# The first stage of an attention and mixture-of-experts layer: the router as moving rows, GpSimd's work later, the first chunk in four loads and banks

## The reference

```
xn = layernorm(x)
out = x + attention(xn) + moe(xn)

attention: q, k, v = xn @ Wq + bq, xn @ Wk + bk, xn @ Wv + bv        (16 heads of 32)
           softmax(q k^T / sqrt(32) + alibi slope * distance, causal) v, then @ Wo + bo
moe:       router_in = norm_w * xn * rsqrt(mean(xn^2) + 1e-6)
           probs = softmax(router_in @ router_w.T)                   (8 experts)
           the two best experts, their shares normalised to 1
           y = 4 * sum over both of share * (silu(xn @ gate) * (xn @ up)) @ down
```

## Time and profile before

| | us |
|---|---|
| median of 3 runs (lowest, highest) | 2081.18 (2076.91, 2083.2) |
| the profiled execution's own time | 2078.22 |
| its span | 2076.2 |
| TensorE busy in the span | 1954.8 |
| VectorE, ScalarE, GpSimd busy | 1442.9, 1320.5, 1360.5 |

### The profile page before, as it was taken

How to read it: one execution, slowest core, us unless ns; L and a number is a source line. 1 busy time by engine, 2 the same in 40 slices (tenths; PEclk the granted TensorE clock), 3 DMA queues, 4 the chain that set the end, 5 groups by cost and what they waited for, 6 DMA issues and landing times. The chain is left out here.

```text
span 2076.2 us, 38386 instructions
## 1 busy us (share of the span) xinstructions
PE 1954.8 (94%) x8670; PEld 1418.8 (68%) x8671; DVE 1442.9 (69%) x3391; ACT 1320.5 (64%) x2603; POOL 1360.5 (66%) x1199
## 2 busy tenths in 40 slices
PE   5999999899999999999999999999969989999996
PEld 4888877666767767676766667677637666666664
DVE  6445455788888888888888888898778833333332
ACT  3323321798998989899898989999852323333332
POOL 4110112788888889888888888888867535555554
PEclk9999999899999999999999999999989999999999
DMA  6667767442423233242423324232117755555554
GB/s 219 213 223 265 240 198 223 122 114 54 120 53 100 74 81 93 68 104 53 103 71 81 94 73 100 53 86 68 34 52 231 229 156 97 99 93 100 95 97 71
DMA packets 118487, 243.94 MB, mean 117 GB/s; under 512 B 15920, under 2 KB 52656, under 8 KB 112144
## 3 DMA queue, kind: packets, MB, share of 16 engines
q1 hardware_dynamic: 100464, 206.09, 34.3%
q0 software_dynamic: 17984, 37.38, 10.3%
HBM read 139.28 MB, written 104.21 MB: 117 GB/s over the span
## 5 line engine op out<-in xcount | busy, mean ns | idle before, releaser
L1061 POOL TENSOR_TENSOR probs_lo<-probs,probs_hi 128x512 fp32r<-128x512 f32 x800 | 1013.5, 1296 | 168.3 <-ACT probs L1092 168.0
L1091 ACT ACTIVATE probs_hi<-s_ps 128x512 fp32r<-128x512 f32 x928 | 597.4, 644 | 93.7 <-DVE s_ps L1155 91.2
L1092 ACT ACTIVATE probs<-s_ps 128x512 f32<-128x512 f32 x960 | 595.5, 651 | 0.2 <-DVE s_ps L1155 0.2
L1134 DVE TENSOR_REDUCE m_part<-m_ps 128x1 f32<-128x512 f32 x744 | 490.7, 684 | 11.3 <-PE m_ps L1369 5.6
L1385 PE MATMUL s_ps<-q_st,k_st 100*128 100x512 f32 (+3 forms) x880 | 323.6, 409 | 35.2 <-ACT probs L1092 17.1
L1369 PE MATMUL m_ps<-k_st,q_st 98*128 98x512 f32 (+2 forms) x840 | 281.7, 377 | 0.0
L1403 PE MATMUL o_ps<-probs_hi,v_split 128*96 128x512 f32 (+3 forms) x748 | 279.0, 383 | 1.0 <-POOL probs_lo L1061 0.5
L1404 PE MATMUL o_ps<-probs_lo,v_split 128*96 128x512 f32 (+3 forms) x748 | 269.9, 364 | 0.0
L1131 DVE CUSTOM_DVE_ANT_0 m_ps<-m_ps,mask_row 128x128 f32<-128x128 f32 x496 | 241.6, 497 | 19.2 <-PE m_ps L1369 12.8
L1385 PEld LDWEIGHTS s_ps<-q_st,k_st 100*128 100x128 f32 x880 | 159.2, 190 | 128.4 <-ACT probs L1092 55.4
L1759 POOL DMA_INDIRECT out<-y,tile_rows x71 | 114.2, 1609 | 170.9 <-issue 99.8
(11 more groups left out here) (202 smaller groups left out, 3615.9 us busy)
## 6 DMA issues: line engine op xcount, KB each, us to landing
v_d<-v_rows SPq DMA_DIRECT2D x7, 3072.0 KB, 9.4
v_split<-v_d SPq DMA_DIRECT2D x22, 768.0 KB, 8.4
k_st<-k_hi_d SPq DMA_DIRECT2D x44, 256.0 KB
q_st<-q_hi_d SPq DMA_DIRECT2D x44, 256.0 KB
xs<-in_x SPq DMA_DIRECT2D x8, 1024.0 KB, 6.8
xn_d<-xs SPq DMA_DIRECT2D x8, 1024.0 KB, 11.4
q_hi_d<-qk_hi SPq DMA_DIRECT2D x32, 256.0 KB, 7.6
q_lo_d<-qk_lo SPq DMA_DIRECT2D x32, 256.0 KB, 7.9
```

Source lines behind the costliest of these rows:

```text
L1061: nc.gpsimd.tensor_tensor(*low_operands(u), ALU.subtract).then_inc(lo_ready_pool, 1)
L1091: nc.scalar.activation(probs_hi[:, P_SLOT[u]], scores, ACT.Exp, scale=SCALE)
L1092: nc.scalar.activation(scores if KIND[u] == "Q" else probs[:, P_SLOT[u]], scores, ACT.Exp, scale=SCALE).then_inc(p_ready, 1)
L1134: V.tensor_reduce(top, scores, AX.X, ALU.max).then_inc(m_taken, 1)
```

## The change

1. The router. `rw` is padded with zeros from 16 to 128 columns and becomes the stationary operand; x moves past it, 512 columns at a time: 4 k x 2 parts = 8 matmuls (`router_rows`). Row n of the result `pr` holds the products with weight column n. DVE copies it to SBUF (`take_rows`; `logit_rows` lies where the raw slopes were, so it waits for `al_ready`), PE turns it back with four transposes (`turn_logits`), and `route` reads the 16 columns of each block. The rows are made ahead of the value tiles and turned behind the second of them; in chunk 7 ahead of tile 4 and tile 6. `route` still follows the value tiles (chunk 7: tile 7 instead of 4).
2. POOL splits Wv, and does all behind it, only once chunk 1's x is normalised.
3. Chunk 0's x comes in four DMAs with a semaphore each; its statistics are taken block by block. Its four transpose groups go to four banks (the maxima's `mp` and the router's `pr` serve as the third and fourth), without waiting for x_lo.

```
-        rw = sb(ctx, "rw", [P, KD, 2 * E], F32R)
+        rw = sb(ctx, "rw", [P, KD, P], F32R)
+        def turned_x(k, first=False):
+            return (xt[:, 0], xt[:, 1], mp[:, :], pr[:, :])[k] if first else xt[:, k % 2]
 SP
-            sp.dma_start(xs[0][:, :, :], x_rows(0)).then_inc(x_loaded[0], 16)
+            for j in range(TPC):
+                sp.dma_start(xs[0][:, j], x[j * P:(j + 1) * P, :]).then_inc(x_first[j], 16)
 POOL
             pool.wait_ge(xn_ready, TPC)
-            for w in range(3):
-                w_low(w)
+            w_low(0)
+            w_low(1)
+            pool.wait_ge(xn_ready, 2 * TPC)
+            w_low(2)
             pool.wait_ge(al_loaded, 16)
 DVE, norm_stats (chunk 0)
                 for j in range(TPC):
+                    if first:
+                        dve.wait_ge(x_first[j], 16)
                     last = nc.vector.bn_stats(stats[:, j], xs[par][:, j])
 DVE
+            def take_rows(c):
+                dve.wait_ge(al_ready, 1)
+                dve.wait_ge(rows_scored, c + 1)
+                nc.vector.tensor_copy(logit_rows[:, :], pr[:, :]).then_inc(rows_taken, 1)
-                nc.vector.tensor_copy(halves[:, :, :], pr[:, 0:TPC * 2 * E].rearrange("p (j e) -> p j e", j=TPC)).then_inc(r_used, 1)
+                nc.vector.tensor_copy(halves[:, :, :], pr[:, :].rearrange("p (j n) -> p j n", j=TPC)[:, :, 0:2 * E]).then_inc(r_used, 1)
+            nc.vector.memset(rw[:, :, 2 * E:].bitcast(F32), 0.0)
 DVE, chunk
                     if last and g == G:
+                        take_rows(c)
+                    if last and g == G + 3:
                         route(c, par)
+                if not last:
+                    take_rows(c)
                 for j in range(TPC):
 PE
-            def router_tiles(c, par):
+            def router_rows(c, par):
+                pe.wait_ge(rw_ready, 1)
                 pe.wait_ge(r_used, c + 1)
+                for k in range(KD):
+                    for n, part in enumerate((x_hi, x_lo)):
+                        last = nc.tensor.matmul(pr[:, :], rw[:, k], part[par][:, k], start=(k == 0 and n == 0),
+                                                stop=(k == KD - 1 and n == 1))
+                last.then_inc(rows_scored, 1)
+            def turn_logits(c):
+                pe.wait_ge(rows_taken, c + 1)
                 for j in range(TPC):
...
+                    last = nc.tensor.transpose(pr[:, j * P:(j + 1) * P], logit_rows[:, j * P:(j + 1) * P], ident)
                 last.then_inc(r_ready, 1)
 PE, chunk
                     if last and g == G:
-                        router_tiles(c, par)
+                        router_rows(c, par)
+                    if last and g == G + 2:
+                        turn_logits(c)
                     qk_tile(c, par, g, first_maxima[g])
-                pe.wait_ge(rw_ready, 1)
+                if not last:
+                    router_rows(c, par)
                 for j in range(TPC):
                     v_tile(c, par, j, first_maxima[2 * G + j])
-                if not last:
-                    router_tiles(c, par)
+                    if not last and j == 1:
+                        turn_logits(c)
```

More of the change, by code:

```diff
@@ L393, in project @@
         rw_ready = sem(ctx, "rw_ready")
+        x_first = [sem(ctx, f"x_first{j}") for j in range(TPC)]
         x_loaded = [sem(ctx, f"x_loaded{p}") for p in range(2)]
@@ L584, in router_root, with x_high @@
                 nc.scalar.activation(rsd[:, :], ms[:, :], ACT.Sqrt).then_inc(rsd_ready, 1)
-            def x_high(c, par, k):
+            def x_high(c, par, k, first=False):
                 act.wait_ge(xt_ready, KD * c + k + 1)
-                nc.scalar.activation(x_hi[par][:, k], xt[:, k % 2], ACT.Copy).then_inc(xh_ready, 1)
+                nc.scalar.activation(x_hi[par][:, k], turned_x(k, first), ACT.Copy).then_inc(xh_ready, 1)
             def qk_high(c, g):
@@ L611, in _ @@
             for k in range(KD):
-                x_high(0, 0, k)
+                x_high(0, 0, k, first=True)
             w_high(1)
@@ L675, in router_scale, with x_low @@
                 inverse_root(rms[:, par], ms[:, :], rsd[:, :])
-            def x_low(c, par, k):
+            def x_low(c, par, k, first=False):
                 dve.wait_ge(xh_ready, KD * c + k + 1)
-                nc.vector.tensor_tensor(x_lo[par][:, k], xt[:, k % 2], x_hi[par][:, k].bitcast(F32),
+                nc.vector.tensor_tensor(x_lo[par][:, k], turned_x(k, first), x_hi[par][:, k].bitcast(F32),
                                         ALU.subtract).then_inc(xl_ready, 1)
@@ L716, in _ @@
             dve.sem_inc(r_used, 1)
-            norm_stats(0, 0)
+            dve.sem_inc(x_loaded[0], 16)
+            norm_stats(0, 0, first=True)
             normalise(0, 0)
             for k in range(KD):
-                x_low(0, 0, k)
+                x_low(0, 0, k, first=True)
             mean_square(0)
@@ L796, in _, with transpose_x @@
         def _(pe):
-            def transpose_x(c, par, k):
+            def transpose_x(c, par, k, first=False):
                 pe.wait_ge(xn_ready, TPC * (c + 1))
-                pe.wait_ge(xl_ready, KD * c + k + 1)
+                if not first:
+                    pe.wait_ge(xl_ready, KD * c + k + 1)
                 for j in range(TPC):
-                    last = nc.tensor.transpose(xt[:, k % 2, j * P:(j + 1) * P], xs[par][:, j, k * P:(k + 1) * P], ident)
+                    last = nc.tensor.transpose(turned_x(k, first)[:, j * P:(j + 1) * P], xs[par][:, j, k * P:(k + 1) * P], ident)
                 last.then_inc(xt_ready, 1)
@@ L843, in v_tile @@
                                                  (x_hi[par][:, k, rows], w_lo[:, 2, k])), maxima)
-            def router_tiles(c, par):
+            def router_rows(c, par):
+                pe.wait_ge(rw_ready, 1)
                 pe.wait_ge(r_used, c + 1)
-                for j in range(TPC):
[L848 to L852, removed]
+                for k in range(KD):
[5 more added lines that the diff above has]
+                pe.wait_ge(rows_taken, c + 1)
+                for j in range(TPC):
+                    last = nc.tensor.transpose(pr[:, j * P:(j + 1) * P], logit_rows[:, j * P:(j + 1) * P], ident)
                 last.then_inc(r_ready, 1)
@@ L856, in _ @@
             for k in range(KD):
-                transpose_x(0, 0, k)
+                transpose_x(0, 0, k, first=True)
             def chunk(c, par, ahead, last=False, first_maxima=((),) * NJ):
```

8 lines of the change are left out of this document (6 added, 2 removed).

## The result

The changed kernel takes 2065.11 us (median of 6 runs, 2061.33 to 2067.41), the kernel before in the same comparison 2082.19 (6 runs, 2076.91 to 2089.19). The ratio is 0.9914, 95% interval 0.9893 to 0.9936, so 13 to 22 us less. Forecast were 2063.3 and a gain. The profiled execution took 2061.33 with a span of 2059.3.

A forecast was written before the change was run, and what follows sets the result against it. TensorE was taken to set the first stage's time, interrupted at the beginning, the gap before chunk 1's x and the router. The terms -10.25 + 2.3 - 5.2 + 3.1 - 7.9 = -17.9 took 2081.2 to 2063.3 us, range 2053 to 2074.

The forecast's parts named there:

- beginning, first projection matmul: Chunk 0: loads in pieces and four banks bring the first projection matmul to near 16.15, -2.5 (bounds -0.5 to -3.5).
- T0 of chunk 1: Chunk 1's first transpose group, within chunk 0: moves from 41.60 to 31.35, -10.25 including the beginning.
- v-end of chunk 0: End of chunk 0's value tiles: -10.25 up to chunk 1's first transposes, then +2.3 for the router's new place.
- chunks 1 to 5: Five chunks from 195.6 to 190.4, -5.2: less TensorE work, but 4.7 of waits at the fourth transpose group.
- chunk 6: Fourth transpose group stays held, so saved router time becomes idle (8 instead of 2.8) with low clock: +3.1.
- chunk 7 to the maximum's transpose: Last chunk: -3.56 and -1.26 from the router and 3.15 of low clock regained, -7.9 (bounds -4.8 to -7.9).
- stages behind it: Everything behind 362 us: nothing changes, carried over whole, 0.
- GpSimd's moved work: Beside chunk 1's ms and rms: x_lo 1 ready at 42.3, before the fourth transpose group at 43.0; 0, otherwise +3.
- the gate: Fourth transpose group waits for x_lo 1, held by q stores queued behind v_d and xn_d: 4.7 in chunks 1 to 5.
- The rival of the low clock at T3: Waits at the fourth transpose group bring low clock, 1.80 lost in three to five chunks: 2071, chance 0.20.
- 3.15 lost to the low clock, which I take back: Chunk 7, from its router's start to tile 5: 9.91 taken where the work makes 6.76; the 3.15 counted as gain.
- no router ahead of it, -3.56: Chunk 7's start: the narrow router's 3.49 and 0.07 of slow following tile no longer stand ahead, -3.56.

The follow-up runs named there:

- e5: Changed kernel with GpSimd's fills and third low part back in their old places; 2131.29 us, ratio to the kernel before 0.9992.
- e0_after: The changed kernel run and profiled once more, no edit; 2118.04 us, ratio to the kernel before 0.9940.
- e4: Changed kernel with chunk 0's x loaded by the one old load and its statistics taken from it; 2122.81 us, ratio to the kernel before 0.9956.
- e1: Kernel before with the new router alone (old first load, two banks, GpSimd's old order); 2127.61 us, ratio to the kernel before 0.9970.
- e6: Changed kernel with every chunk's v_d store sent in two halves; 2057.05 us, ratio to the kernel before 0.9875.
- e3: Kernel before with its 32 narrow router matmuls moved ahead of the value tiles, chunk 7 unchanged; 2097.27 us, ratio to the kernel before 1.0068.
- e7: Changed kernel with head 0's loads behind chunk 6's fourth q store pair, head 1's behind all chunk 7's stores; 2068.18 us, ratio to the kernel before 0.9929.
- e0_before: The kernel before run and profiled once more, no edit; 2132.27 us, ratio to the kernel before 1.0003.
- group B: Follow-up runs on one chip of their own, compared only among themselves; the kernel before took 2081.56 us there (median of 17 runs).
- group C: Follow-up runs on another chip of their own, compared only among themselves; the kernel before took 2132.57 us there (median of 18 runs).
- group A: Follow-up runs on another chip of their own, compared only among themselves; the kernel before took 2130.92 us there (median of 26 runs).
- e2: Changed kernel with the old router of 32 narrow matmuls in its old place; 2121.57 us, ratio to the kernel before 0.9951.

## Why the prediction was right or wrong

Against the steps, by the first profile (v-end of chunks 0, 5 and 6 at 59.20, 250.60 and 300.50):

| step | forecast | measured |
|---|---|---|
| beginning, first projection matmul | -2.5 | -2.71 (18.67 to 15.96) |
| T0 of chunk 1 | -10.25 | -10.21 (41.60 to 31.39) |
| v-end of chunk 0 | -7.95 | -8.27 |
| chunks 1 to 5 | -5.2 | -4.2 (195.6 to 191.4) |
| chunk 6 | +3.1 | +3.2 (46.72 to 49.90) |
| chunk 7 to the maximum's transpose | -7.9 | -1.5 (51.97 to 50.46) |
| the stage | -17.9 | -10.8 |
| stages behind it | 0 | -6.1 in this pair of profiles |

**Right.** The start of the stage, to 0.3. It was right for the reason given: e5 takes GpSimd's move away and gets 3.27 and 4.81 back on VectorE and T0 at 41.82. Two numbers inside were wrong without harm. I had T0 wait 2.25 and it waited 3.95, as TensorE made tile 0 in 2.9 instead of 4.35; in e0_after, where tile 0 took 4.27, it waited 2.14. And I had written that without the low clock behind T0 2.0 more would be gained. In e0_after and e4 it was absent, and T3 came no sooner, for x_lo 1 came late behind GpSimd's memsets. So GpSimd's moved work, which I had priced at 0, is hidden only behind the low clock's cost, and costs 1.2 without it.

**Right: where the router's gain goes.** I had not counted TensorE's 9.9 for chunks 1 to 5 but about half of it, as x_lo at T3 hangs on q stores behind 4 MB of others. The waits are there (3.7, forecast as 4.7), the router alone brings 0.7 in e1, and e6 removes the gate and the waits with it. One sum on the way is wrong: 4.6 MB at 400 GB/s take 11.5 us, not the 15 that I set beside them. From 71.0 to 86.4 the DMA engines moved 316 GB/s on average, which makes 4.9 MB; near 400 was reached only from 74 to 83. Chunk 6 came to 0.1 of its figure. The rival of the low clock at T3 fell: with waits of 0.26 to 1.13 in chunks 1 to 5 the mean clock of each 40 us from 60 to 260 is 1.00. (My remark that no idle time as short as 1.4 was followed by the low clock was stronger than the rows: the first four projection matmuls of the kernel before took 2.07 after 1.50 idle, where the changed kernel's took 1.20 after 1.50; the granted clock of both windows reads 1.00, so what made the difference is open.)
The rule of the Trainium skill on which that rival leaned ("TensorE: Matmul & The Clock Gate", HAM oscillation — how this bites in real kernels) speaks of waits of several microseconds; the trace agrees for 3.71 and 8.52. Nearest to 1.4 is a wait of 1.38 at T3 of chunk 5 in e0_after, and full clock followed it.

**Wrong: chunk 7.** The step that failed is "3.15 lost to the low clock, which I take back" together with "no router ahead of it, -3.56". Both savings were made on TensorE, and a new wait took most of them: 3.71 at 330.56, and the low clock that follows it (330.56 to 335.72 is 5.2, for a tile of 2.80 and three maxima matmuls of 0.23, 3.5). In chunk 7 I asked only about TensorE's clock. I had reckoned in chunk 6 that what TensorE saves becomes idle time where a store holds it, and did not follow SP's queue one chunk further, where head 1's loads stand behind xn_d and in front of the q stores. The two savings together bring TensorE to the store some 8 us sooner, and the store doesn't land sooner. e3 tells them apart: with the first alone (-3.5) chunk 7 takes 48.42 and TensorE waits 0.87; with the wide router and the clock taken back as well it takes 50.46 in the changed kernel and 50.54 in e1 (51.38 in e0_after). So the narrow router and the low clock behind it had been cover, and taking them away cost 2 or more instead of giving 4.4. My bounds for the step (-4.8 to -7.9) both took TensorE's side of it. e7 shows the cause in SP's queue: with the loads of both heads behind the stores the wait goes and chunk 7 takes 44.10, 7.9 less than before. The figure was right for a chunk without this queue.

**The total was hit with help.** The stage missed by 7.1 us, and 6.1 of it came from stages in which both kernels run the same instructions. That this made up for the miss is luck. From s to the end of the span takes 1754.6 in e0_before and 1755.1 in e0_after; in the first profiles and group B it takes 1700.1 to 1708.6, with the first profile of the changed kernel, the fastest of its six runs, at the low end, and in group C 1753.2 to 1762.6. So it is scatter as far as traces go. What stays open: against the median of before in its group, every version but e5 has 0.3 to 6.4 less time than its s explains (e3 too, which is slower). The traced executions of the kernel before were 4.0 (first profile) and 3.3 (group A) under its median, which would make up for about as much; whether those other executions lose their time in the first stage no trace shows. The change is worth 9 to 11 us by the stage and 13 to 17 by what the two intervals of its ratio have in common.

## What to carry to other kernels

When a step shortens the busiest engine's work between two transfers, follow the queue of transfers to the end of the stage, not to the next wait: what was cover here was needed in seven chunks, and in the last one even a stretch at the low clock had been cover. The gain of the router lay nearly unused until the 3 MB store was halved and fourteen loads were put behind the stores that compute waits for; those edits, a few lines each, brought 20 to 23 us in the stage, twice the change itself. And a load can be late as well as early: moved too far, it took back all that it had given (e7).

## What was not expected of the hardware

- The half clock stood behind narrow matmuls while TensorE was busy: in e2 at 101 to 103, behind the router of chunk 1 (TensorE busy 2.00 of 2.00, DMA 402 GB/s), and not behind the router of chunk 0. In e3, where only their place differs from the kernel before, it stood in every stretch of 40 us, and with the wide router (after, e1) in none from 60 to 260. Why behind some narrow routers and not others is open.
- The length of a wait alone doesn't tell what follows: 2.14, 2.17 (e0_after, e4) and also 3.26 (e0_before, 292.75, granted 1.00 to 297.7) were followed by full clock, 2.82 at the same place and 3.95 by half.
- Four loads of 256 KB landed at about 3.5 (two), 5.4 and 6.4, one of 1 MB at 6.26; in this pair of profiles the last piece came 0.15 later and the weights behind it 1.0.
- `output` takes 170 us or more in groups A and C and about 120 elsewhere, for the same kernel. In e0_before TensorE stands 11.97 us there in front of one group of eight matmuls with nothing that the profile shows as its releaser, and 15.94 for VectorE's sums; what sets it apart is open.
